# Packing Q for the scores of a decoder layer: one wait for both halves of its high part, and the six transfers ordered by row instead of by half

## The reference

```python
Q = proj(query, Wq, bq)        # 16 heads of 8 columns
K = proj(key, Wk, bk)
V = proj(value, Wv, bv)
scores = jnp.einsum('bhqd,bhkd->bhqk', Q, K) * sm_scale
attn = jax.nn.softmax(scores, axis=-1)
ctx = jnp.einsum('bhqk,bhkd->bhqd', attn, V)
```

## Time and profile before

| | us |
|---|---|
| median of 3 runs | 630.23 |
| lowest and highest run | 629.39, 632.25 |
| the profiled execution, its own time | 630.23 |
| its span, first to last instruction | 627.5 |
| PE busy | 598.9 |
| DVE, POOL, ACT busy | 495.1, 479.9, 451.6 |

### The profile page before, as it was taken

How to read it: one execution, slowest core, us unless ns; L and a number is a source line. 1 busy time by engine, 2 the same in 40 slices (tenths; PEclk the granted TensorE clock), 3 DMA queues, 4 the chain that set the end, 5 groups by cost and what they waited for, 6 DMA issues and landing times.

```text
span 627.5 us, 31020 instructions
## 1 busy us (share of the span) xinstructions
PE 598.9 (95%) x13344; PEld 440.7 (70%) x13344; DVE 495.1 (79%) x1279; ACT 451.6 (72%) x831; POOL 479.9 (76%) x619
## 2 busy tenths in 40 slices
PE   9999999999999999999999999999999999996774
PEld 7776767767677777767677777767676777574664
DVE  2555677787888888888888888888888888879887
ACT  3636566978778696978778796978878796957642
POOL 5424154888889889898889889898889888898744
PEclk9999999999999999999999999999999999999577
DMA  8203222364454727264535637265535735344500
GB/s 332 70 19 98 93 66 83 48 153 71 129 89 129 121 87 146 60 158 87 129 88 121 131 83 150 60 158 88 127 88 120 131 79 119 85 99 87 104 18 33
DMA packets 116153, 64.87 MB, mean 103 GB/s; under 512 B 94321, under 2 KB 100850, under 8 KB 115890
## 3 DMA queue, kind: packets, MB, share of 16 engines
q1 hardware_dynamic: 116018, 62.91, 43.4%
HBM read 17.27 MB, written 4.19 MB: 34 GB/s over the span
## 4 chain that ended last, share of the span: by engine, by line
PE 77%; ACT 6%; DVE 5%; DMA 4%; SPq 4%; issue 2%; POOL 1%; POOLq 0%; DVEq 0%; ACTq 0%
PE bank L337 17%; PE bank L327 10%; PE bank L357 9%; PE bank L449 4%; PE bank L318 3%; DMA pack<-Ql 3%; PE bank L414 3%; SPq L1296 3%; PE bank L435 2%; PE bank L284 2%; PE bank L295 2%; PE bank L492 2%; ACT qT L577 2%; PE bank L512 2%; PE bank L513 2%
## 5 line engine op out<-in xcount | busy, mean ns | idle before, releaser
L337 PE MATMUL bank<-Mh,GT 128*32 128x128 f32 x4096 | 128.3, 274 | 0.0
L337 PEld LDWEIGHTS bank<-Mh,GT 128*32 128x32 f32 x4096 | 107.1, 110 | 20.8 <-issue 17.8
L918 DVE TENSOR_REDUCE mx<-bank 128x8 f32<-128x512 f32 x128 | 79.1, 682 | 19.4 <-PE bank L414 19.4
L665 ACT ACTIVATE PT<-bank 128x512 f32<-128x512 f32 x128 | 64.4, 625 | 33.5 <-PE bank L435 33.5
L327 PE MATMUL bank<-kp,xs 64*128 64x512 f32 x256 | 76.2, 626 | 0.0
L1191 POOL TENSOR_TENSOR gall<-gall,lnr 128x512 f32<-128x512 f32 x56 | 73.1, 1315 | 1.4 <-DVE st L853 1.4
L550 ACT ACTIVATE Cb<-bank 128x512 f32<-128x512 f32 x81 | 48.4, 598 | 33.3 <-PE bank L337 29.2
L550 ACT ACTIVATE GT<-bank 128x512 f32<-128x512 f32 x95 | 50.5, 600 | 29.3 <-PE bank L327 26.7
L1196 POOL TENSOR_TENSOR gs<-gall,gs 128x512 f16<-128x512 f32 x56 | 64.0, 1162 | 8.2 <-ACT gs L702 8.2
L1135 POOL TENSOR_TENSOR rstd<-ve,mhalf 128x4 f32<-128x4 f32 x60 | 63.8, 1063 | 5.0
L598 ACT ACTIVATE x<-x,nmr,rstd 128x128 f32<-128x128 f32 x120 | 50.1, 512 | 19.3 <-POOL nmr L1150 19.2
(11 more groups left out here) (203 smaller groups left out, 1565.5 us busy)
## 6 DMA issues: line engine op xcount, KB each, us to landing
pack<-Qh SPq DMA_DIRECT2D x64, 128.0 KB, 2.6
xT<-in_xT SPq DMA_DIRECT2D x16, 256.0 KB, 3.4
xs<-in_x_nat SPq DMA_DIRECT2D x16, 256.0 KB, 2.8
cxT<-in_cxT SPq DMA_DIRECT2D x16, 256.0 KB, 3.8
Kp<-Kh SPq DMA_DIRECT2D x32, 128.0 KB, 2.1
pack<-Ql SPq DMA_DIRECT2D x32, 128.0 KB, 2.6
out_y<-yo SPq DMA_DIRECT2D x15, 256.0 KB, 2.4
Kp<-Kl SPq DMA_DIRECT2D x16, 128.0 KB, 2.2
```

The costliest lines, as they stand in the source:

```text
L337: m = e.matmul(bk[32 * j:32 * j + 32, tile(g_)], GT[b % 4][:, tile(hh, 32)], Mh[:, tile(hh)], start=True, stop=True)
L665: e.activation(PT[tp][:, tile(j, 512)], bank[uses["prob", s, i][0]][:, :], ACT.Exp, scale=SM).then_inc(emptied("prob", s, i)[0], 1)
L918: e.tensor_reduce(to, bank[uses["score", s, i][0]][:, :].rearrange("p (g b k) -> p g b k", g=2, b=4), AX.X, ALU.max).then_inc(emptied("sco ...
```

## The change

`qpack` waits once for both halves of `Qh`, and its three kinds of rows are the outer loop: first row 0 for the two halves, then row 2 for the two halves, then, behind the same wait as before, the `Ql` row for the two halves. The same six DMAs write the same places. No other function changes, and the order of the instructions of the other engines stays the same.

```diff
-                for i in two:
-                    w.wait_ge(s_qh, 2 * s + 1 + i)
-                    for r in (0, 2):
-                        e.dma_start(Qp[p][4 * i + r:128:8, :], Qh[64 * i:64 * i + 64, :]).then_inc(s_qp[p], 16)
-                w.wait_ge(*emptied("qproj", s))
-                for i in two:
-                    e.dma_start(Qp[p][4 * i + 1:128:8, :], Ql[64 * i:64 * i + 64, :]).then_inc(s_qp[p], 16)
+                w.wait_ge(s_qh, 2 * s + 2)
+                for r, src in ((0, Qh), (2, Qh), (1, Ql)):
+                    if r == 1:
+                        w.wait_ge(*emptied("qproj", s))
+                    for i in two:
+                        e.dma_start(Qp[p][4 * i + r:128:8, :], src[64 * i:64 * i + 64, :]).then_inc(s_qp[p], 16)
```

## The result

The changed kernel takes 639.37 us (median of 4 runs, 638.40 to 640.41) against 630.16 (median of 4 too; a fourth run was added to the three above): the ratio of the runs is 1.0141, with a 95% interval of 1.0117 to 1.0165, which is 7.4 to 10.4 us. It is slower by 1.4%. The forecast was 638.0, in a range of 633.5 to 641.0. The difference of the two medians is 9.2 us. Beside the experiments the kernel before ran 15 and 24 times more, with medians of 631.59 and 631.42, and against those it would be 7.8 and 8.0. So the effect is some 8 to 9 us, and isn't known closer.

The account below looks back on a forecast made before the run. PE's work plus its waits for the last `Ql` transfer was taken to bound the kernel. 6.4 + 1.3 + 0.1 = 7.8 us gave a span of 635.3, and with 2.7 us around it 638 us, range 633.5 to 641.0.

Parts of the forecast that it names:

- The bound: Loop: PE's work plus its waits, chiefly for the last `Ql` transfer ahead of the scores, going one for one into periods.
- The start 0.70 us later: SP's first `Qh` transfer: waits for the second half, so starts 0.69 to 0.70 us later, as do the DMAs behind it.
- The order at nothing: SP's six transfers: alternating between the halves costs nothing, as two issues take 0.62 us each against 0.63.
- The collisions: Trains meeting PE's instruction fetches: fetch time fixed, long issue one place earlier, landing 0.64 us later; bound 0.70.
- The rival of the escape: Later trains escape fetch stalls: 627.0 us if all do, chance 0.04; three groups or some more, 633 to 636, 0.12.
- Group 14, 0.1, and group 15, nothing: Last two groups: 14 pays 0.1 us beyond a wait for ACT's copy; 15 nothing, as DVE reads first scores at 581.55.
- The sum: All groups: ten at 0.64 make 6.4 us, groups 5, 6 and 10 make 1.3, group 14 0.1; together 7.8 us.

Follow-up runs that it names:

- experiment 3: Changed kernel, with all six transfers also waiting until DVE has made `Ql`, 1.54 us later still: 665.25 us (2 runs).
- experiment 5: PE's and ACT's `qproj` moved ahead of q2 and q3: 627.46 us on the kernel before (0.9935 of it), 629.66 on the changed one (0.9980).
- experiment 1: Changed kernel's new transfer order without the late start, first transfer waiting for the first half alone: 630.54 us, 0.9992 of the kernel before.
- experiment 2: Old transfer order, but one wait for both halves of `Qh` ahead of all six: 639.86 us, 1.0149 of the kernel before.
- experiment 4: Step c6 moved ahead of `score0` in PE's plan: 634.51 us on the kernel before (1.0063 of it), 636.19 on the changed one (1.0076).
- experiment 6: Kernel before with 32 more dummy matmuls at the start of PE's list (57 instead of 25), moving the fetches: 637.56 us (one run).

## Why the prediction was right, point by point

*The bound.* Right: PE's waits for the trains, and nothing else in the loop, with 1:1 into the periods. Experiments 3 and 5 carry it: without room the whole wait goes into the period, with room nothing does.

*The start 0.70 us later.* Right (159.75 against 159.05 for the end of the first half), and experiments 1 and 2 put the whole cost on it.

*The order at nothing.* Right (experiment 1). The section of the Trainium skill that the prediction weighed here, "Anatomy of one DMA — SWDGE (gpsimd) path" of the page DMA: Bandwidth & Descriptors, is on transfers that GpSimd issues, and these are SP's; the point rests on the experiment.

*The collisions.* The step that was mis-sized. The prediction held the fetches fixed in PE's program, so that the long issue comes one place earlier and a group pays 0.64. It does come earlier, second to fourth in ten of the twelve groups of the loop, where it was fourth to sixth, but by one to three places and not always by one; in groups 3 and 9 it stayed where it was. Group 1, free of a fetch before, now met one and waited 0.2 us. One train, that of group 6, in SP's timeline:

```profile
267.78 3.40 SPq L1298 DMA_DIRECT2D pack<-Qh  x4
271.23 1.23 SPq L1298 DMA_DIRECT2D pack<-Ql  x2
```

The fetches jitter by up to some 1 us from one execution to the next, so single groups paid anything from 0.15 (group 8) to 1.3 us (group 6, 7.23 us from first issue to scores where PE was there after 5.97). The mean cost of a collision in groups 2 to 13 is the same 0.94 us before and after, so the landings moved by 0.70 in the mean and not by 0.64, and the twelve groups paid 7.9 us instead of the 7.1 of the sum. That the two means agree so well is luck: in the six kernels of experiments 1, 2, 4 and 5 they run from 0.86 to 1.19, so the loop's share can come out a us or more off in a single execution.

*The rival of the escape.* It didn't happen: not one of the trains of groups 2 to 13 escaped. In experiment 3, at 2.2 us, six of the twelve did. The Trainium skill's page Runtime: NRT & Kernel Launch, section "Instruction fetch mechanics", calls the cost of a block "mostly hidden". The section says nothing of the transfers of another queue, so the prediction read more into it than it states; there the cost is 0.94 us of each train in the mean. For PE, which executes the block, the traces agree in the main: of the 105 packets of q8 in the kernel before, two are followed by an idle stretch of PE that no wait explains (0.58 and 0.16 us). But it isn't always hidden. In experiment 6 PE's waits have the row

```profile
PE bank L449 <- issue: 2.5, 2, 1.8
```

In the ten profiles, from 60 us on, there are 17 such gaps of 0.16 to 1.8 us, and 16 of them end 2.3 to 3.2 us after a fetch began. That the fetch causes them is argued from its place and was not tested. Between the kernel before and the changed one they make at most 0.7 us, and none lies between 98 and 550 us.

*Group 14, 0.1, and group 15, nothing.* Group 14 is right: from its first issue to that of group 15 it is 28.66 us before and 28.74 after. Group 15 at nothing is the step that failed, by 0.7 us in the two profiles and by 1.3 in the mean of the kernels below. The prediction looked at DVE's reading of the first scores, which indeed begins as before (7.5 and 7.6 us after the first half of `Qh`), and took that for the path. It left out the transposes of g that SP issues behind the train. The chain that ended last runs over DVE's maxima before, and over the first of these transposes after (start, us, what; before, then after):

```profile
585.75 0.69 DVE mx L918
...
586.57 0.41 PE bank L422
...
587.06 0.28 ACT Mrow L550
```

```profile
588.10 4.63 DMA gT<-gs
...
592.81 0.63 ACT gs L702
593.44 1.54 ACT x L598 x4
...
595.04 0.28 ACT Mrow L550
```

From the first half of `Qh` (574.1 and 581.5) ACT's copy of the turned maxima, `Mrow`, comes 13.0 us later before and 13.6 after, and from there to the end of the span it is 40.4 and 40.5 us. So these 0.6 us are nearly the whole of the 0.7. PE waits for the same transpose, ahead of the step that turns the maxima (L422). Its first matmul on it, before and after:

```profile
584.51 0.27 PE L512 MATMUL bank<-tpj,gT 128*128 128x128 f16 x1 [2.65 <-DMA gT<-gs]
```

```profile
592.87 0.27 PE L512 MATMUL bank<-tpj,gT 128*128 128x128 f16 x1 [2.88 <-DMA gT<-gs]
```

From the first half of `Qh` of group 15 these are 10.4 and 11.4 us, though SP issued the transpose at the same distance (6.5 and 6.6): it took 3.8 us to land before and 4.6 after. This goes with the place of the next fetch. In all four kernels with the start 0.70 us late a block is fetched 8.8 to 9.3 us after that half, and this matmul comes after 11.3 to 11.4 us; in the four with the early start and the usual dummies the fetch is at 7.4 to 7.7 and the matmul at 10.4 to 10.8. In both the fetch falls while the transpose is under way, and no run moved the fetch alone, so that it is the cause isn't shown. The turn of the maxima comes 0.5 us later in the mean of the four late ones. In the kernel of experiment 6, whose trains start early, the fetch is at 8.1, the matmul at 11.6 and the end from that half on is 54.7 us, longer than in any of the eight; so the end can be as long without the late start.

In the mean of four and four the end from there is 1.3 us longer (53.7 against 52.4 us), and what is left of it goes with the granted clock, whichever the start: 0.81 and 0.82 in the last stretch of the two late kernels whose rows stand above, 0.84 and 0.88 in that of the two early ones, but 0.88 also in the late one of experiment 2, whose last stretch is 81.9 us, shorter than that of the kernel before:

```profile
553.04:634.90 81.86, 56.14 (x1094) 45.09 (x1090) 68.23 (x198) 44.93 (x85) 56.13 (x83) 0.88 0.31 71
```

Why the clock is low for longer in some of them wasn't tested, and stays open.

*The sum.* 7.8 us forecast; 7.9 in the loop, 0.7 in the end and -0.6 ahead of group 2 by the profile; 9.2 by the medians. Without the 1.1 us that this execution was ahead at group 0 the profile would give 9.1. The sum took 0.64 for group 0, which paid 0.8. The mechanism and the loop were forecast rightly; that the loop's 7.9 lies so near the 7.8 of the whole sum is chance, since the loop's share of that sum was 7.1.

## What to carry to other kernels

A wait that is always met where it stands in an issuing queue costs nothing there, and can cost much further ahead. Moving it ahead of the first of six transfers delayed all six by one ACT instruction, 0.70 us, and PE, which had 0.7 us of room for an undisturbed train and hardly any for the others, paid most of it: 7.9 us in the twelve groups of the loop. Ask of each hand-over how much room it has against the consumer when the transfer is disturbed, and not only when it is not. Where it has none, give it room in the order of the producers, as putting `qproj` ahead of two steps that could wait did (0.65% faster than before), rather than in the consumer's, where 1.0 us of room cost 0.6 us a period.

## What the runs showed of the hardware that was not expected

- A block of PE's instructions fetched while SP issues transfers goes with one of SP's issues taking 0.3 to 1.7 us beyond its 0.6, or, where it comes late in the train, with a late landing; each of the 131 trains that met one landed late, by 0.3 to 2.0 us, and experiment 6 moved the long issue by moving the fetch.
- The fetches keep their place in PE's list only within about 1 us from one execution to the next, so a single group proves nothing. Means over twelve groups agreed to 0.05 us between before and after, but run from 0.86 to 1.19 us over the other kernels with the usual dummies and a start at most 0.7 us late.
- PE's clock stayed at full through waits of 1.2 us in the loop and through those of up to 1.9 us in experiment 3; there it fell to half for a moment at five of seven waits of 2.0 to 2.8 us, which cost another 1.4 to 1.6 us in each of the two periods shown.
- PE itself stood idle for 0.16 to 1.8 us, with no wait that the profile shows, 17 times in ten profiles; 16 of these gaps end 2.3 to 3.2 us after the start of a fetch.
